# A fused transformer block on one core: the scores of a head pair issued in two stages, with a projection between them

## The reference, cut to what matters

```python
def attn_layer(x, Wqkv, qs, ksc, Wo):            # 16 heads of 64, window 32
    q, k, v = split(x @ Wqkv)
    q = l2norm(q) * qs;  k = l2norm(k) * ksc
    q = q * cos * scale + rotate_half(q) * sin * scale
    k = k * cos * inv + rotate_half(k) * sin * inv
    sim = einsum('bhwie,bhwje->bhwij', bq, bk2) * QK_SCALE   # each window sees itself and the one before
    attn = softmax(where(mask, -max, sim), -1)
    out = einsum('bhwij,bhwje->bhwie', attn, bv2)
    return out @ Wo
for i in range(6):
    x = attn_layer(shift_tokens(x), ...) + x
    x = ffn_layer(shift_tokens(x), ...) + x      # layer norm, W1, a * gelu(gate), W2
```

## Time and profile before

| what | value |
|---|---|
| time of the profiled execution | 3555.15 us |
| its span, first to last instruction | 3553.3 us |
| median of three runs | 3560.82 us |
| PE matmul busy | 3325.9 us (94% of the span), 65032 matmuls |
| DVE, ACT, POOL busy | 77%, 72%, 57% |
| mean granted TensorE clock | 0.984 of full speed |
| DMA | 423.34 MB, mean 119 GB/s |

### The profile page before, as it was taken

How to read it: one execution, slowest core, us unless ns; L and a number is a source line. 1 busy time by engine, 2 the same in 40 slices (tenths; PEclk the granted TensorE clock), 3 DMA queues, 4 the chain that set the end, 5 groups by cost and what they waited for, 6 DMA issues and landing times.

```text
span 3553.3 us, 149054 instructions
## 1 busy us (share of the span) xinstructions
PE 3325.9 (94%) x65032; PEld 2107.6 (59%) x65032; DVE 2737.3 (77%) x3420; ACT 2545.5 (72%) x5866; POOL 2041.5 (57%) x1557
## 2 busy tenths in 40 slices
PE   7999987999999999999999999999999999999996
PEld 3444434666666666666666666666666666666663
DVE  3656557888887878888788878788888878788883
ACT  4667655777777777777777767677777777787774
POOL 0000006766676666766666666667676667676661
PEclk9999998999999999999999999999999999999998
DMA  3223224333333333433333333334333333333330
GB/s 109 76 71 84 75 61 141 135 127 127 134 133 133 118 127 130 140 131 129 119 122 136 130 124 127 127 124 143 126 130 126 121 136 125 135 127 131 129 122 24
DMA packets 247337, 423.34 MB, mean 119 GB/s; under 512 B 71966, under 2 KB 110108, under 8 KB 246556
## 3 DMA queue, kind: packets, MB, share of 16 engines
q1 hardware_dynamic: 220368, 397.28, 33.1%
q10 hardware_dynamic: 26316, 16.52, 1.6%
HBM read 124.21 MB, written 7.34 MB: 37 GB/s over the span
## 4 chain that ended last, share of the span: by engine, by line
PE 64%; DVE 17%; issue 7%; ACT 5%; POOL 5%; DMA 1%; SPq 1%; DVEq 0%; POOLq 0%; ACTq 0%
PE PS L535 64%; DVE TPB L932 5%; DVE MX L956 2%; ACT SC L1237 1%; DVE NV L947 1%; POOL K L1324 1%; POOL Q L1342 1%; DMA RB<-root_scratch 1%; POOL K L1342 1%; DVE PP L977 1%; DVE PX L978 1%; DVE NV L945 1%; DVE H L800 1%; DVE H L1000 1%; DVE NV L949 1%
## 5 line engine op out<-in xcount | busy, mean ns | idle before, releaser
L932 DVE SCALAR_TENSOR_TENSOR TPB<-PS,VEC,C 128x1024 f32<-128x1024 f32 x768 | 961.8, 1270 | 102.0 <-ACT SX L1213 95.0
L1237 ACT ACTIVATE SC<-PS,BQ,RQ 128x64 f32<-128x64 f32 x3072 | 979.5, 436 | 40.7 <-DVE BQ L961 40.3
L1213 ACT ACTIVATE SX<-PS 128x512 f32<-128x512 f32 x768 | 461.5, 620 | 391.4 <-PE PS L535 388.4
L1324 POOL TENSOR_TENSOR K<-K,RB 128x512 f32<-128x512 f32 x384 | 497.2, 1295 | 283.1 <-DMA RB<-root_scratch 278.4
L1347 POOL TENSOR_TENSOR SC<-SC,RC 128x1024 f32<-128x1024 f32 x192 | 366.3, 1908 | 480.2 <-DVE RC L969 478.8
L535 PEld LDWEIGHTS PS<-PP,VV 32*64 32x64 f32 x24576 | 433.7, 133 | 278.6 <-issue 276.3
L535 PE MATMUL PS<-PP,VV 32*64 32x64 f32 (+1 forms) x24576 | 541.2, 223 | 7.8 <-issue 6.2
L1342 POOL TENSOR_TENSOR K<-TPB,TR 128x512 f32<-128x512 f32 x384 | 496.4, 1293 | 0.0
L1342 POOL TENSOR_TENSOR Q<-TPB,TR 128x512 f32<-128x512 f32 x384 | 495.5, 1290 | 0.0
L535 PE MATMUL PS<-LXH,LH 128*128 128x512 f32 x768 | 371.3, 484 | 85.2 <-DVE TPB L932 68.4
L535 PE MATMUL PS<-K,Q 64*32 64x64 f32 (+1 forms) x24576 | 302.2, 224 | 49.5 <-issue 48.0
(11 more groups left out here) (167 smaller groups left out, 5809.8 us busy)
## 6 DMA issues: line engine op xcount, KB each, us to landing
TR<-TPB SPq DMA_DIRECT2D x768, 256.0 KB, 2.7
RB<-root_scratch SPq DMA_DIRECT2D x768, 128.0 KB
PP<-PX SPq DMA_DIRECT2D x192, 192.0 KB, 2.6
WS<-in_wqkv ACTq DMA_DIRECT2D x72, 128.0 KB, 2.4
PP<-PX SPq DMA_DIRECT2D x192, 48.0 KB, 2.5
QA<-TH SPq DMA_DIRECT2D x128, 64.0 KB, 2.1
QA<-TL SPq DMA_DIRECT2D x128, 64.0 KB, 2.1
KA<-TH SPq DMA_DIRECT2D x128, 64.0 KB, 2.1
```

The source lines that it names most:

```text
L932: e.scalar_tensor_tensor(TPB[:, n % 3:4 + n % 2:3 + n % 2 - n % 3, w, :], g, VEC[:, l, 9 + w:10 + w], C[:, at:at + 1024].rearrange("p (o c ...
L1213: e.activation(SX[i % 3][:, :], bk("PJ", key)[:, :], ACT.Square).then_inc(sem["pj_act"], 1)
L1237: p = e.activation(SC[m % 2][:, g, :, :].rearrange("p x k -> p (x k)"), bank[s][:, at:at + 64], ACT.Exp, bias=BQ[m % 2][:, g:g + 1], scale ...
L1324: e.tensor_tensor(dst, dst, RB[n % 2][:, :], ALU.mult).then_inc(sem["pr_pool"], 1)
```

## The change

Three things are changed. First, S1 is two stages. S1 of (m, 0) puts the mask into the banks and computes the first head pair's scores; S1 of (m, 1) computes the second's. The first waits for one `pr_pool` step less than before. The places -0.250 and -0.074 put the key projection at -0.132 between them. Second, in the last unit the output projection's parts are no longer at the end: they follow the values of each m. Third, all places are set anew.

```diff
-    "LS": 221.000, "LB": -1.200, "LO": -0.800, "S1": -0.074, "MX": 0.116, "S3": (0.544, 0.762, 0.998, 1.143),
+    "LS": 220.103, "LB": -1.638, "LO": -0.499, "S1": (-0.250, -0.074), "MX": 0.151,
+    "S3": (0.619, 0.761, 0.955, 0.965), "SU": 1.459, "NP": 1.207, "TT": 2.273, "PX": 2.418,
...
-        lay(z + P["WO"][0], group, "WO", u, "wo_dve", 2 * u + 2)
+        wo = P["WO"]
+        if u == NB * DEPTH - 1:
+            wo = [max(P["F5"] - 7.99, 2 * i + P["PVn"] + 0.6) for i in range(4)]
+        lay(z + wo[0], group, "WO", u, "wo_dve", 2 * u + 2)
         for i in range(1, 4):
-            lay(z + P["WO"][i], o.put, "WOp", u, i)
+            lay(z + wo[i], o.put, "WOp", u, i)
...
-            for st in ("S1", "MX", "SU", "NP", "TT", "PX", "PVn"):
+            for st in ("MX", "SU", "NP", "TT", "PX", "PVn"):
                 lay(n + P[st], o.put, st, m)
+            for i in range(2):
+                lay(n + P["S1"][i], o.put, "S1", m, i)
...
-                    m, = key
-                    for name, value in [] if m else o.first:
-                        on.wait_ge(name, value)
-                    if m:
-                        on.wait_ge("s3_act", 4 * m)
-                    for r in range(4):
-                        for s in range(2):
-                            k = slice(64 * s, 64 * s + 64)
-                            at = 64 * s + 32 * (r > 0)
-                            mm(bank[s][32 * r:32 * r + 32, :], identb[k, at:at + 32], maskb[k, :], True, False, skip_group_check=True)
-                    on.wait_ge("pr_pool", 2 * m + 2)
-                    for hp in range(2 * m % 8, 2 * m % 8 + 2):
+                    m, x = key
+                    hp = 2 * m % 8 + x
+                    if x == 0:
+                        for name, value in [] if m else o.first:
+                            on.wait_ge(name, value)
+                        if m:
+                            on.wait_ge("s3_act", 4 * m)
+                        for r in range(4):
+                            for s in range(2):
+                                k = slice(64 * s, 64 * s + 64)
+                                at = 64 * s + 32 * (r > 0)
+                                mm(bank[s][32 * r:32 * r + 32, :], identb[k, at:at + 32], maskb[k, :], True, False, skip_group_check=True)
+                    on.wait_ge("pr_pool", 2 * m + x + 1)
+                    for c in range(4):
...
+                    if x == 1:
+                        p.then_inc(sem["s1_pe"], 1)
```

More of the change, by code:

```diff
@@ L720, in tensor_program @@
-                    p.then_inc(sem["s1_pe"], 1)
+                    m, x = key
[10 more added lines that the diff above has]
+                                mm(bank[s][32 * r:32 * r + 32, :], identb[k, at:at + 32], maskb[k, :], True, False, skip_group_check=True)
@@ new lines, in tensor_program @@
+                    on.wait_ge("pr_pool", 2 * m + x + 1)
+                    for c in range(4):
+                        for r in range(4):
+                            j = 4 * c + r
+                            first = 0 if j else 32
+                            at = 256 * x + 64 * c
+                            for s in range(2):
+                                p = mm(bank[s][32 * r:32 * r + 32, at + first:at + 64],
+                                       Q[64 * s:64 * s + 64, hp, 32 * j:32 * j + 32],
+                                       K[64 * s:64 * s + 64, hp, 32 * j - 32 + first:32 * j + 32], False,
+                                       x == 1 and j > 11, skip_group_check=True)
```

## The result

The changed kernel takes 3597.68 us (median of 4, 3593.24 to 3603.46) where the kernel before takes 3557.99 (median of 4): a ratio of 1.0112, with a 95% interval of 1.009 to 1.0135. It is slower by about 40 us, against a forecast of 3596.

The account below looks back on a forecast made before the run. PE was taken to bound the layers most of the time. Terms of 0.55 + 0.65 + 0.1 + 0.05 - 0.5 = 0.85 us per unit, times 47, plus 0.5, took 3555.15 to 3596 us; 8-in-10 range 3525 to 3635.

Parts of the forecast that it names:

- The maximum waits for the projection in between: At m mod 4 = 3, MX starts later because DVE handles the in-between projection first: 0.55 us per unit (0 to 0.65).
- The mask waits earlier: S1's mask, now ahead of the projection, waits for ACT's S3 of the m before: 0.65 us per unit (0 to 1.2).
- and so inherit the 1.08 us: At m = 97, ACT's first exponentials wait for BQ, so S3 takes on the 1.08 us by which MX is later.
- the signs named ahead: Profile after: later MX, DVE's wait for PE replaced by TPB's, SC waits 20 to 50 us, issue waits 45 to 75.
- under 10 us: Forecast wrong if PE's waits for SC stay under 10 us; the time would then be near or under 3555.
- Change-overs: Extra small-to-full tile change per m on PE, 0.15 us, less 0.09 for the moved key projection: +0.05 per unit counted.
- Fetch gaps: PE's instruction-fetch stalls in the scores: sum unchanged, but about half hidden under other waits, -0.5 us per unit.
- rival of fetch relief: Score gaps on PE vanish because the in-between projection lets fetching catch up: -48 us, about 3530 us in all; chance 0.25.
- m mod 4 = 0: Mask waits another 0.1 us per unit here (0 to 0.45), as F1 and ACT's copies behind it come later.
- The last unit: Output projection spread behind the values of each m: same work, idle time +0.7, so +0.5 us (-3 to +2).
- full price: Mask waits of 1.2 us in every unit and 0.45 at m mod 4 = 0, nothing back: 122 us, 3677; chance 0.05.
- All hidden: TPB and S3 delays fall where PE already waits for DVE, so time stays at 3550 to 3565; chance 0.15.

## Why the prediction was right, point by point

That the split makes the kernel slower, and by about 40 us, is shown twice: by doing it alone, and by undoing it in the changed kernel. But that the sum of 40.5 us met the measured 40 is in good part luck. The two largest terms, 26 us for the late maximum and 31 for the mask, are waits, and the runs show few of them; the term for PE's own work, 2 us, is really 26 to 29, and the fetch gaps gave back 12 us, not 23.5.

*The maximum waits for the projection in between: the delay came, its cause mostly not.* Forecast 0.55 us per unit, 26 in all, at m mod 4 = 3. Splitting only there costs 0.72%, or 26 us; the profiled executions differ by 16.6 (spans 3569.9 and 3553.3). MX starts later, counted from the end of the values and averaged over 44 units, by 0.46 us there (3.51 to 3.97), and in the changed kernel by 0.43. But counted from the end of the last score it starts 0.05 us behind it before and 0.24 with the split at 3. So only 0.2 us of the delay is the wait for the projection in between; in the rest MX is late because the scores themselves end later. In the changed kernel this lag is 0.25, and with both halves put back it is 0.24: there the split adds nothing to it and still costs 37 us.

Nor does PE wait longer behind that maximum. From the end of the scores of m mod 4 = 3 to the end of the next ones its waits for DVE fall, from 36.5 to 17.4 us, in the run with 3 alone. (In the changed kernel its waits for TPB there are 48.6 us, but with both halves put back they are 50.3.) What grows is PE's own time: 9 us between the values and the end of the scores of 3, and 10 us in RQ and F2 behind them, besides 7.6 us in which F2, which stood behind 136 score matmuls and now stands behind 64, waits for ACT's H. The forecast missed all three. PE comes later and MX comes later, side by side, and which of the two sets the end was not separated: no run moved F1 and F2 alone. So the cost of this part is shown, and its price as a wait is not.

*The mask waits earlier: right in kind and place, too large.* Forecast 0.65 us per unit at m mod 4 = 2, 31 in all; measured by stage 12.4 us there in the changed kernel (2.6 before). The wrong step is "and so inherit the 1.08 us", and the value of 0.65 taken from it. The 1.08 us is the delay of MX in one m; the mean of m mod 4 = 1 is +0.75 (3.32 to 4.07). Of that, S3 has at its start +0.56 (5.66 to 6.22) and at its end +0.47 (11.25 to 11.72), and against the end of the values ahead of the next mask it is +0.26 (-0.14 to +0.12), since PE comes later itself. At m = 97 BQ takes up most of it: it takes 1.26 us before (1554.07 to 1555.33) and 0.42 after, and both times ends as POOL's operation does (below). Of the signs named ahead, issue waits of 45 to 75 us came (53.4) and so did the shift from "MX <- PE" to TPB; the waits for SC, said to be 20 to 50 us, are 15.4 over the span and 9.0 from 620 to 3440. By the second count the sign "under 10 us" spoke against the forecast, and the time near 3555 that it was to go with did not come.

*Change-overs: the step that failed worst.* "Only those outside the waits above count: +0.05 per unit." The 0.15 us per cut was right: the score stages' time on PE, waits taken out, grows by 7.5, 8.5, 4.6 and 7.4 us for m mod 4 = 0 to 3, 28 us in all or 0.15 per m. But it was not hidden in waits: in 1 and 2 the mask waits that were to do so are mostly not there, and it is some 13 us; in 0 and 3, 15. And the saving set against it, the moved key projection, came as 7 us less busy time (3325.9 to 3318.6 in the run with that move alone) and as 41 us more of waits for TPB. That a cut costs time is measured; that it does so because the array changes between small and full tiles is an inference.

*Fetch gaps: "no change in their sum" was wrong by 12 us.* 65.0 us in 80 pieces became 53.4 in 74 (whole span), from the splits at 1 and 2. The forecast said the gaps would be hidden, not shorter, and put -23.5 us for it; the trace shows -12, on PE itself. How the gaps came to be shorter stands in the last part. The rival of fetch relief had the right sign, and a quarter of its 48 us.

*m mod 4 = 0:* forecast 5 us; what is left of the split alone (1.21%) when 3 (0.72%) and 1 and 2 (0.29%) are taken off is 0.20%, 7 us, within the intervals of the three. *The last unit:* +0.5 forecast; +0.05% (-0.07 to +0.16) alone. In the changed kernel's trace the last quarter waits for its copy as forecast:

```profile
3542.41 1.98 PE L540 MATMUL PS<-AOT,LO 128*128 128x512 f32 x4
...
3547.70 3.59 PE L540 MATMUL PS<-AOT,LO 128*128 128x512 f32 x4 [1.12 <-ACT AOT L1257]
```

1.12 us of waiting, and 3.59 us for four matmuls that take 1.98 elsewhere, at a granted clock of 0.53 in that stretch, which the forecast did not have.

So for m mod 4 = 1 and 2 together the forecast had 31 of mask waits, 2 of change-overs and 23 coming back; measured with only these split are 14 more of mask waits (2.5 before, 16.1), about 14 of change-overs, and 15 less of fetch gaps (65.0 to 49.9), together some 13, where the runs give 0.29% or 10 us: nearly the same net, by other parts.

*Slips in the working that the result did not turn on.* PE is busy 530 of 580 us in the attention block, which is 91%; 98% is not the share of the block. The two kinds of wait are 117.5 of the 136 us; a third, 14.5 us for DVE's H, is not named. Half of "full price" is 61 us and gives 3616, not 3630. The last S3 part moved in 36 of 192 m, twice "one in ten", and gave nothing.

*The rivals.* "All hidden" fell (the interval begins at 0.9%), and so did "full price". Open stays why the move of the key projection costs 0.46% alone and nothing that can be told beside the split. A guess, not tested: it makes PE arrive earlier at projections that DVE releases, and with the split DVE is late there already.

No version tried beats the kernel before by more than the measurement can tell; the nearest is the split at m mod 4 = 2 alone, 0.9995.

## What to carry to other kernels

When a stage is put between two others on one engine, look at the in-order queue of each engine that reads them: here the maximum came no earlier with the scores split, since it needs both halves and another projection's rotary products stand ahead of it, and putting it first made PE wait for an accumulator and the kernel 12% slower than before. Cutting a run of small matmuls in two has a price in PE's own work, which the trace shows only as longer stages, never as a wait; measure it by stage, and undo one part of the change at a time before reading "busy" and "idle" of the whole. A place in a table of numbers means nothing without its neighbours: -0.250 cost 0.9% in one table and 3.0% in the other. And a total that comes out as forecast is no proof of its terms: look for each term where it was said to be.

## What the runs showed of the hardware

*PE stalls at one position of a block of 256 instructions.* In the traces of the kernel before, of the changed one and of all runs with a result, each of PE's "issue" gaps over 0.15 us, 58 to 87 in a kernel, stands at instruction 192 or 193 of a block of 256 in PE's own list (two for each matmul, and the others counted). That fits instruction fetches in the 16 KB packets of the earlier trace rows. The gaps also go with how fast PE came from one such position to the next:

| time from one such position to the next | before: times, with a gap, us of gaps | changed: the same |
|---|---|---|
| under 2 us | 18, 15, 18.8 | 1, 1, 1.6 |
| 2 to 3.3 us | 101, 39, 31.4 | 112, 57, 41.9 |
| 3.3 to 4 us | 69, 27, 15.9 | 38, 9, 4.6 |
| over 4 us | 320, 0, 0 | 357, 7, 5.4 |

(66.0 us in all before, with one gap ahead of RQ, and 53.4 after.) So the split shortened the gaps with no instruction less: the blocks that ran in under 2 us are all but gone, and somewhat more blocks of 2 to 3.3 us stall instead, as the forecast had it; only the balance came out at -12 us and not at zero. A fixed time of 3.3 us for a block is too simple, since many blocks of 2 to 3.3 us have no gap and a few over 4 us have one.

*DVE's small BQ waits for POOL.* It takes from 0.17 to 1.34 us, with a mean of 0.72 at m mod 4 = 0 before. At m = 97 in the kernel before it ends at 1555.33, and POOL's operation in that trace at 1555.29:

```profile
1554.03 1.26 POOL L1342 TENSOR_TENSOR Q<-TPB,TR 128x512 f32<-128x512 f32 x1
1554.07 1.26 DVE L961 SCALAR_TENSOR_TENSOR BQ<-MX,RQ 128x16 f32<-128x16 f32 x1
```

and in the changed kernel at 1568.98, POOL's at 1568.96:

```profile
1567.67 1.29 POOL L1349 TENSOR_TENSOR Q<-TPB,TR 128x512 f32<-128x512 f32 x1
...
1568.91 1.27 POOL L1349 TENSOR_TENSOR K<-TPB,TR 128x512 f32<-128x512 f32 x1
```

The Trainium skill, "SBUF — State Buffer", section "SBUF: two separate sides", describes an exclusive lock that a DVE operation with two SBUF inputs and a POOL operation that reads SBUF take in turn, each for its whole length; these rows agree. BQ ends within 0.08 us of the end of a POOL operation in 75 to 98% of the m of each class, in both kernels. A delay ahead of such an operation can vanish in it, as here, or grow by a whole POOL operation.
